# A two-layer transformer kernel: first-stage row stores on GpSimd's queue with three expert buffers, and one 33-row bias product per block

## The reference

```
x = x + L0_attn(layernorm(x), ...)      # 16 heads, bias min(rel * slope, 8), softmax
x = x + L0_xattn(layernorm(x), ctx, mask, ...)
x = x + L0_ffn(layernorm(x), ...)       # top 2 of 8 experts, per sequence
x = x + L1_attn(layernorm(x), ...)      # attends over the 4 sequences at one position
x = x + L1_xattn(layernorm(x), ctx, ...)
x = x + L1_ffn(layernorm(x), ...)       # top 2 of 8 experts, per row
```

## Time and profile before

| | us |
|---|---|
| median of three runs | 3141.96 (3135.05 to 3144.26) |
| the profiled execution | 3139.22 |
| its span in the profile | 3137.4 |
| first stage (`constants`) | 0 to 101.9 |
| first mixture (`mixture0`) | 1293.8 to 1340.7 |
| second self-attention (`attention1`) | 1357.2 to 1460.3 |

### The profile page before, as it was taken

How to read it: one execution, slowest core, us unless ns; L and a number is a source line. 1 busy time by engine, 2 the same in 40 slices (tenths; PEclk the granted TensorE clock), 3 DMA queues, 4 the chain that set the end, 5 groups by cost and what they waited for, 6 DMA issues and landing times. The chain is left out here.

```text
span 3137.4 us, 38375 instructions
## 1 busy us (share of the span) xinstructions
PE 2805.0 (89%) x12634; PEld 1764.7 (56%) x12634; DVE 1855.2 (59%) x3754; ACT 1302.2 (42%) x2326; POOL 1662.9 (53%) x1406
## 2 busy tenths in 40 slices
PE   5688886999999999587999999999999999999979
PEld 5344445555565665454656556665656556556557
DVE  2466766665767665446555556556556555556456
ACT  1155564444455455122444444444444444444410
POOL 2144403665666667502466666666666666666710
PEclk8789998999999999797999999999999999999979
DMA  8655613232332321002223232224222233222110
GB/s 278 132 152 163 157 33 109 64 102 51 103 75 54 97 63 32 34 0 73 60 69 74 53 99 68 52 68 106 53 67 68 54 97 75 57 63 63 32 54 27
DMA packets 114229, 245.51 MB, mean 78 GB/s; under 512 B 16239, under 2 KB 62576, under 8 KB 112881
## 3 DMA queue, kind: packets, MB, share of 16 engines
q1 hardware_dynamic: 107824, 219.52, 27.4%
q0 software_dynamic: 5696, 23.42, 2.7%
q10 hardware_dynamic: 512, 0.13, 0.0%
HBM read 106.98 MB, written 31.80 MB: 44 GB/s over the span
## 5 line engine op out<-in xcount | busy, mean ns | idle before, releaser
L1049 POOL TENSOR_TENSOR ACC<-ACC,PR 128x512 f32<-128x512 f32 (+1 forms) x1056 | 1331.0, 1282 | 456.2 <-ACT PR L1274 448.2
L1274 ACT ACTIVATE PR<-banks 128x512 f32<-128x512 f32 (+1 forms) x832 | 468.8, 597 | 669.2 <-PE banks L1163 668.2
L1335 DVE TENSOR_REDUCE mx<-banks 128x2 f32<-128x800 f32 (+1 forms) x512 | 504.1, 986 | 393.6 <-PE banks L1115 392.0
L1179 PE MATMUL banks<-PR,V 128*64 128x512 f32 (+1 forms) x2496 | 599.1, 604 | 0.0
L1162 PE MATMUL banks<-QA,KA 128*128 128x512 f32 (+1 forms) x1248 | 535.5, 429 | 12.3 <-DMA QB<-ROW 11.5
L1115 PE MATMUL banks<-KH,QZ 128*128 128x400 f32 (+1 forms) x1536 | 480.7, 372 | 41.2 <-DVE mx L1335 20.8
L1163 PE MATMUL banks<-QB,KB 65*128 65x512 f32 (+1 forms) x1248 | 495.2, 397 | 0.0
L1115 PEld LDWEIGHTS banks<-KH,QZ 128*128 128x128 f32 x1536 | 267.9, 189 | 225.6 <-issue 89.7
L1274 ACT ACTIVATE PR<-banks,small 128x512 f32<-128x512 f32 (+1 forms) x416 | 269.4, 687 | 300.3 <-PE banks L1163 290.1
L1332 DVE CUSTOM_DVE_ANT_0 banks<-banks,maskadd 128x400 f32<-128x400 f32 (+1 forms) x512 | 289.2, 588 | 143.6 <-PE banks L1115 136.8
L1303 DVE TENSOR_TENSOR KB<-banks,KH 64x400 fp32r<-64x400 f32 (+1 forms) x384 | 219.4, 571 | 260.0 <-ACT KH L1207 254.5
(11 more groups left out here) (243 smaller groups left out, 2977.4 us busy)
## 6 DMA issues: line engine op xcount, KB each, us to landing
KA<-KH SPq DMA_DIRECT2D x192, 400.5 KB
CX<-ctx_split SPq DMA_DIRECT2D x8, 2403.0 KB, 10.4
WK<-wk_split SPq DMA_DIRECT2D x48, 256.0 KB, 5.7
WV<-wv_split SPq DMA_DIRECT2D x24, 512.0 KB, 3.9
QA<-QZ SPq DMA_DIRECT2D x96, 128.0 KB
QB<-QZ SPq DMA_DIRECT2D x96, 128.0 KB
first<-in_w_in SPq DMA_DIRECT2D x8, 1024.0 KB, 6.2
second<-in_w_out1T SPq DMA_DIRECT2D x8, 1024.0 KB, 8.8
```

The source lines that it names most:

```text
L1049: pool.tensor_tensor(acc, other, PR[0:r, n % RING, :], ALU.add).then_inc(summed, 1)
L1179: last = pe.matmul(OB[h * DH:(h + 1) * DH, :], V[0:r, g % 4, s, h * DH:(h + 1) * DH], PR[0:r, (n + h) % RING, :], start=(s == 0), stop=(s ...
L1274: act.activation(PR[0:r, n % RING, :], SB[n % 3][0:r, :], ACT.Exp, bias=keybias[0:r, g // pairs, t:t + 1] if masked else 0.0).then_inc(pro ...
L1335: dve.tensor_reduce(mx[:, :, t, c], couples[i % 2 if g == 0 else 0][:, :, 0:w], AX.X, ALU.max).then_inc(mx_done, 1)
```

## The change

In the first stage the `tab` load and the ten row stores are issued by GpSimd instead of SyncE; `tab` ahead of the `relb` iotas, the stores behind the selects. The two zeroings go behind the stores, and the row of zeros is then stored from the zeroed `QS`, so `nil` goes. The expert buffers become three pairs: load e waits for expert e - 3, and store e - 3 follows load e in SyncE's order. In the second self-attention the two one-row products per block become one over 33 rows: row 0 of `row_hl` holds the high half, row 32 the low half, the rows between are zeros, and `one_hi` has 33 rows of ones. For that the bias vectors are loaded twice, into partitions 0 and 32, and GpSimd has more to do in the first mixture.

```diff
-                         (self.row1[:, 0:3 * C], row("b1_in")), (self.row1[:, 3 * C:4 * C], row("b1_out"))):
+                         (self.row1[0:1, 0:3 * C], row("b1_in")), (self.row1[0:1, 3 * C:4 * C], row("b1_out")),
+                         (self.row1[32:33, 0:3 * C], row("b1_in")), (self.row1[32:33, 3 * C:4 * C], row("b1_out"))):
...
                 def load_expert(e):
-                    if e >= 2:
-                        sp.wait_ge(ready, e - 1)
+                    if e >= 3:
+                        sp.wait_ge(ready, e - 2)
...
                 load_expert(0)
                 load_expert(1)
+                load_expert(2)
                 sp.dma_start(self.X[:, :, :], a["x"].rearrange("b (t p) c -> p (b t) c", p=P)).then_inc(x_in, 16)
...
-                sp.wait_ge(tabled, 2 * H + NT + 1)
-                sp.dma_start(tab[:, :], table[:, :, :]).then_inc(tab_in, 16)
-                sp.wait_ge(cleared, 4)
-                sp.wait_ge(dstep, 7)
...
-                for e in range(2, E1):
+                for e in range(3, E1):
                     load_expert(e)
-                    store_expert(e - 2)
+                    store_expert(e - 3)
+                store_expert(E1 - 3)
                 store_expert(E1 - 2)
                 store_expert(E1 - 1)
...
+                pool.wait_ge(tabled, 2 * H + NT + 1)
+                pool.dma_start(tab[:, :], table[:, :, :]).then_inc(tab_in, 16)
                 for h in range(BANDS):
                     pool.iota(relb[:, h, :], [[1, P]], base=int(CLAMP[h]), channel_multiplier=-1,
                               allow_small_or_imprecise_dtypes=True).then_inc(related, 1)
...
-                pool.memset(raw(self.QS[:, :, :]), 0.0).then_inc(zeroed, 1)
-                pool.memset(raw(self.KS[:, :, :, :]), 0.0).then_inc(zeroed, 1)
...
+                pool.wait_ge(cleared, 3)
+                pool.dma_start(k_rows[14], one[:, :]).then_inc(z_out, 16)
+                pool.wait_ge(dstep, 7)
+                for i in range(2):
+                    pool.dma_start(k_rows[NT * i:NT * (i + 1)].rearrange("t h n -> (t h) n"), raw(ZK[:, i, :])).then_inc(z_out, 16)
+                    pool.dma_start(k_rows[8 + 3 * i:11 + 3 * i].rearrange("t h n -> (t h) n"), raw(ZK[0:3 * H, 2, :])).then_inc(z_out, 16)
+                pool.wait_ge(dstep, 13)
...
+                pool.memset(raw(self.QS[:, :, :]), 0.0).then_inc(zeroed, 1)
+                pool.memset(raw(self.KS[:, :, :, :]), 0.0).then_inc(zeroed, 1)
+                pool.wait_ge(zeroed, 4)
+                pool.dma_start(q_rows[14], raw(self.QS[0:H, 0, :])).then_inc(z_out, 16)
+                pool.wait_ge(z_out, 16 * 10)
...
-                dve.memset(nil[:, :], 0.0).then_inc(cleared, 1)
...
-                link(pool.tensor_tensor(row[:, 0:3 * C], row[:, 0:3 * C], self.gam1[0:1, :], ALU.mult))
-                link(pool.tensor_tensor(row[:, 3 * C:4 * C], row[:, 3 * C:4 * C], self.gam2[0:1, :], ALU.mult))
-                link(pool.tensor_copy(self.row_hi[:, :], row[:, :]))
-                link(pool.tensor_tensor(self.row_lo[:, :], row[:, :], raw(self.row_hi[:, :]), ALU.subtract))
-                link(pool.tensor_copy(self.one_hi[:, :], self.ones[0:1, :]))
+                hl, hi = self.row_hl, self.row_x
+                link(pool.memset(raw(hl[:, :]), 0.0))
+                for r in (0, 32):
+                    link(pool.tensor_tensor(row[r:r + 1, 0:3 * C], row[r:r + 1, 0:3 * C], self.gam1[r:r + 1, :], ALU.mult))
+                    link(pool.tensor_tensor(row[r:r + 1, 3 * C:4 * C], row[r:r + 1, 3 * C:4 * C], self.gam2[r:r + 1, :], ALU.mult))
+                link(pool.tensor_copy(hl[0:1, :], row[0:1, :]))
+                link(pool.tensor_copy(hi[32:33, :], row[32:33, :]))
+                link(pool.tensor_tensor(hl[32:33, :], row[32:33, :], raw(hi[32:33, :]), ALU.subtract))
+                link(pool.tensor_copy(self.one_hi[:, :], self.ones[0:33, :]))
...
-                    pe.matmul(J, self.one_hi[:, :], self.row_hi[:, o:o + n], start=False, stop=False)
-                    return pe.matmul(J, self.one_hi[:, :], self.row_lo[:, o:o + n], start=False, stop=True)
+                    return pe.matmul(J, self.one_hi[:, :], self.row_hl[:, o:o + n], start=False, stop=True)
...
-                            pe.matmul(J, self.one_hi[:, :], self.row_hi[:, 3 * C:4 * C], start=False, stop=False)
-                            last = pe.matmul(J, self.one_hi[:, :], self.row_lo[:, 3 * C:4 * C], start=False, stop=True)
+                            last = pe.matmul(J, self.one_hi[:, :], self.row_hl[:, 3 * C:4 * C], start=False, stop=True)
```

More of the change, by code:

```diff
@@ L146, in middle_room @@
         self.alpha = sb("alpha", [P, CK])
-        self.row1 = sb("row1", [1, 4 * C])
-        self.row_hi = sb("row_hi", [1, 4 * C], F32R)
-        self.row_lo = sb("row_lo", [1, 4 * C], F32R)
-        self.one_hi = sb("one_hi", [1, P], F32R)
+        self.row1 = sb("row1", [33, 4 * C])
+        self.row_hl = sb("row_hl", [33, 4 * C], F32R)
+        self.row_x = sb("row_x", [33, 4 * C], F32R)
+        self.one_hi = sb("one_hi", [33, P], F32R)
     def norm_all(self, HTA, Hn, ahead=None, low=None):
@@ L238, in constants @@
             one = tmp("one", [H, S])
-            nil = tmp("nil", [H, S])
             work = tmp("work", [TH, 3, S])
@@ L243, in constants @@
             KF = F1 // P
-            first = [tmp(f"first{i}", [P, KF, C]) for i in range(2)]
-            second = [tmp(f"second{i}", [P, KF, C]) for i in range(2)]
+            first = [tmp(f"first{i}", [P, KF, C]) for i in range(3)]
+            second = [tmp(f"second{i}", [P, KF, C]) for i in range(3)]
             parts = tmp("parts", [P, 2, 2, CK * C], F32R)
-            we_in = [sem("w_in0"), sem("w_in1")]
+            we_in = [sem("w_in0"), sem("w_in1"), sem("w_in2")]
             we_out = [sem("w_out0"), sem("w_out1")]
@@ L258, in load_expert @@
                 def load_expert(e):
-                    if e >= 2:
-                        sp.wait_ge(ready, e - 1)
-                    sp.dma_start(first[e % 2][:, :, :], a["w_in1"][e].rearrange("(k p) n -> p k n", p=P)).then_inc(we_in[e % 2], 16)
-                    sp.dma_start(second[e % 2][:, :, :], a["w_out1T"][e].rearrange("(k p) n -> p k n", p=P)).then_inc(we_in[e % 2], 16)
+                    if e >= 3:
+                        sp.wait_ge(ready, e - 2)
+                    sp.dma_start(first[e % 3][:, :, :], a["w_in1"][e].rearrange("(k p) n -> p k n", p=P)).then_inc(we_in[e % 3], 16)
+                    sp.dma_start(second[e % 3][:, :, :], a["w_out1T"][e].rearrange("(k p) n -> p k n", p=P)).then_inc(we_in[e % 3], 16)
                 def store_expert(e):
@@ L297, in _ @@
                     sp.wait_ge(we_out[i], 16 * E1 // 2)
-                sp.wait_ge(z_out, 16 * 10)
                 sp.wait_ge(x_in, 16 * 6)
@@ L327, in _ @@
                                            base=lim, pattern=[[0, P]], channel_multiplier=-1).then_inc(made, 1)
+                k_rows, q_rows = self.k_rows, self.q_rows
+                pool.wait_ge(cleared, 3)
[5 more added lines that the diff above has]
+                pool.wait_ge(dstep, 13)
+                for i in range(2):
+                    pool.dma_start(q_rows[NT * i:NT * (i + 1)].rearrange("t h n -> (t h) n"), raw(ZQ[:, 0, :])).then_inc(z_out, 16)
+                    pool.dma_start(q_rows[8 + 3 * i:11 + 3 * i].rearrange("t h n -> (t h) n"), raw(ZQ[0:3 * H, 1 + i, :])).then_inc(z_out, 16)
+                pool.memset(raw(self.QS[:, :, :]), 0.0).then_inc(zeroed, 1)
[3 more added lines that the diff above has]
+                pool.wait_ge(z_out, 16 * 10)
             @block.scalar
@@ L347, in _ @@
                 for e in range(E1):
-                    pe.wait_ge(we_in[e % 2], 32 * (e // 2 + 1))
+                    pe.wait_ge(we_in[e % 3], 32 * (e // 3 + 1))
                     if e >= 4:
@@ L352, in _ @@
                         for k in range(KF):
-                            last = pe.matmul(bank[e % 4][:, m * C:(m + 1) * C], first[e % 2][:, k, m * P:(m + 1) * P],
-                                             second[e % 2][:, k, :], start=(k == 0), stop=(k == KF - 1))
+                            last = pe.matmul(bank[e % 4][:, m * C:(m + 1) * C], first[e % 3][:, k, m * P:(m + 1) * P],
+                                             second[e % 3][:, k, :], start=(k == 0), stop=(k == KF - 1))
                     last.then_inc(ready, 1)
@@ L1489, in _ @@
                     pool.tensor_tensor(X[:, t, :], X[:, t, :], Hn[:, t, :], ALU.add).then_inc(based, 1)
-                pool.wait_ge(self.att1_in, 16 * 7)
+                pool.wait_ge(self.att1_in, 16 * 9)
                 for k in range(CK):
```

10 lines of the change are left out of this document (removed).

## The result

The changed kernel takes **3113.1 us** (median of 4 runs, 3107.8 to 3116.1) where the kernel before takes 3142.0 us in the same comparison: **ratio 0.991, 95% interval 0.9896 to 0.9924**. A second comparison on another occasion gave 3113.1 us (6 runs) and 0.9911 [0.9895, 0.9927]. The profiled execution took 3112.4 us (span 3110.6). So the forecast of 3115 us held, and 3113 lies inside the range; but none of its three terms came out right for quite the reasons given, and their errors partly cancelled, as the stages show.

The account below looks back on a forecast made before the run. Bounds: late expert loads in the first stage, PE and VectorE in the mixture, TensorE up to a ScalarE copy in the second self-attention. Gains 16.9 + 9.1 - 0.7 = 25.3 us from 3139.2 and 3142.0 gave 3115 us, range 3105 to 3127.

Parts of the forecast that it names:

- 16.9 us forecast: First stage: it would end at 85.0 us instead of 101.9, a gain of 16.9 us, bounds 12.0 to 19.0.
- the stream brings one with its store each 7.9 us, so PE is not the bound: First stage: transfers need 7.9 us per expert with its store, TensorE 7.17 us, so transfers set the pace.
- my 72.3: First stage: the last expert's load would land at 72.3 us (70.2 to 75.5), the mixed transfers taken at 330 GB/s.
- 0.7 us lost forecast: Mixture stage: added GpSimd work would slow a VectorE product on the path by 0.7 us, bounds nothing to 2.34.
- What I called the third: Mixture stage: the VectorE `wbg` product starting at 1325.67 us, claimed to run beside GpSimd after the change.
- 9.1 us forecast: Second self-attention: one bias product per block instead of two gains 7.7 us up to a ScalarE copy plus 1.4 us.
- The bound that I had worked out from the columns alone: Second self-attention: lower bound if only the columns' time is saved, 20 x 0.11 + 10 x 0.22, plus 4 x 0.2: 5.2 us.
- the second step: Second self-attention: TensorE's last four output blocks, at the low clock, each save 0.36 us, 1.4 us together.
- One (holes in the stream): First stage: SyncE's waits come late for each expert, leaving queue holes; only 10 us won there, 3121 us; chance 0.12.
- two (nothing from the product): Second self-attention: the new bias product saves nothing, as weight loads or VectorE's sums set the pace; 3123 us; chance 0.06.
- four (`tab` behind the backlog): First stage: `tab` on GpSimd's queue waits behind SyncE's backlog; stage gains 11 us, 3120 us; chance 0.04.
- Three (the low clock all through the stage): First stage: TensorE stays at the low clock, 14.3 us an expert, stage 27.6 us later, 3158 us; chance 0.03.

Follow-up runs that it names:

- after_again: The changed kernel itself, nothing altered, run and traced once more: 3113.1 us, ratio 0.9911 against the kernel before.
- first_only: The changed kernel with the two one-row bias products brought back, so only the first stage is new: 3120.9 us, ratio 0.9933 against before.
- one_row: The changed kernel with a one-row bias product, the high half alone, the low half left out: 3108.4 us, one run.
- x_late_again: Second run of the changed kernel with six other loads (X, w, wout, biases) moved behind the experts' loads: 3104.0 us, ratio 0.9885 against before.
- bias_only: The changed kernel with the old first stage brought back, so only the bias product is new: 3133.4 us, ratio 0.9971 against before.
- x_late_q: The changed kernel with six other loads behind the experts' loads and the second self-attention's projection bias for the query half alone: 3105.2 us, ratio 0.9889 against before.

## Why the prediction was right, point by point

**First stage: 16.9 us forecast, 18.8 measured; the steps around it right, the bound wrong.** As said: the gap before the third expert gone, a gap of 7.1 (forecast 8.5) before the fourth, table steps from 8.3 us, nine of the ten row stores issued by 18.4, zeroings done by 32.2 (forecast 37), no wait at the rows, queue never empty before 70 us, and a tail of 83.1 - 70.6 = 12.5 us behind the last expert's first product (77.51 - 6.9 = 70.6), forecast 12.7. The failed step is "the stream brings one with its store each 7.9 us, so PE is not the bound". I took 330 GB/s for the mixed part; it ran at 359 to 377 GB/s from 30 to 65 us, where the experts' loads alone had 348, so 2.62 MB took some 7.2 us. The trace of before had shown it, in windows that I left out for one in which the transfers were not always busy (70 to 75 us): here loads beside a store,

```profile
45.00:50.00 5.00, 5.00 (x20) 4.19 (x19) 0.00 (x0) 0.00 (x0) 0.00 (x0) 0.77 1.10 357
```

and 361 GB/s from 40 to 45 us. TensorE needs 6.9 us for an expert inside a run; the 7.17 us that I used is one expert by itself. With rates so near each other the one that starts late decides, and that was TensorE: it had nothing to do from 33.02 to 40.15 us, the granted clock was 0.51 and 0.50 (the low level, 1.2 GHz) from 35 to 45 us, and expert 3 took 9.8 us, as the split behind it shows (ScalarE at 49.92 us). The last expert's second load, issued at 57.23 us and 11.3 us under way, was there at 68.5 us, 3.8 us before my 72.3; TensorE came to it at 70.6. So my stream was too slow by 3.8 us, and 2.1 us of that were lost again because TensorE came late. Expert 3's 2.9 us over the 6.9 cover that: it is the clock, which I had left out. (The gain itself is uncertain by the 1.5 us between the two traces of the old stage.)

**Mixture: 0.7 us lost forecast; about 0.95 lost, on another product, and hidden in the trace by the clock.** The stage has four `wbg` products. What I called the third, at 1325.67 us, is the fourth; the true third was hit:

```profile
1296.91 1.79 POOL L1501 TENSOR_TENSOR row<-row,gam 1x768 f32<-1x768 f32 x1
...
1297.62 2.16 DVE L1571 TENSOR_TENSOR wbg<-wb,small 128x1024 f32<-128x1024 f32 x1
1298.78 1.59 POOL L1502 TENSOR_TENSOR row<-row,gam 1x256 f32<-1x256 f32 x1
1299.84 3.32 PEld L1517 LDWEIGHTS banks<-wbg,wa 128*128 128x128 f32 x16 [3.26 <-DVE wbg L1571]
```

It starts inside GpSimd's 1.79 us and takes 2.16 us instead of 1.21; GpSimd's next, started inside it, takes 1.59 us instead of the 0.72 of the same line four microseconds later. The same pair in the trace of before, where the product began as the multiply ended:

```profile
1314.80 1.79 POOL L1496 TENSOR_TENSOR row<-row,gam 1x768 f32<-1x768 f32 x1
...
1316.58 1.21 DVE L1565 TENSOR_TENSOR wbg<-wb,small 128x1024 f32<-128x1024 f32 x1
1316.67 1.70 POOL L1497 TENSOR_TENSOR row<-row,gam 1x256 f32<-1x256 f32 x1
```

So there the two already met, and only GpSimd paid (1.70 us). The 33-row memset moved the multiply later against VectorE's product. The one that I had named began at 1307.66 us, as the subtract had ended at 1307.65, and took 1.22. My mistake was to skip this product and to lay the new work behind the old in time without sliding the old multiplies themselves. That whichever of the two starts first holds the pair of ports and the other waits is what "SBUF — State Buffer" of the Trainium skill (SBUF: two separate sides) says, and this trace agrees: 0.95 us more, where 1.08 us of the multiply were left. The stage's length, with its norm, fell all the same, from 62.69 to 62.05 us, because TensorE's last L1517 block (L1511 before) ran at the full clock (3.72 us, before 5.41). I don't count that as the change's doing: in after_again, the same kernel, the stage takes 66.20 us. Nor is the 0.95 us a fixed price. In the twelve traces with the longer GpSimd list this product takes from 1.22 to 2.16 us, in after_again 1.30: there TensorE's blocks ahead of it, and with them the product, came later against GpSimd's list, and a later GpSimd multiply paid (2.67 us instead of 1.80).

**Second self-attention: 9.1 us forecast, 7.9 measured; the mechanism right, the size taken at the wrong end.** Up to the resume I had 7.7 us, from the distance between the two products' starts, 0.22 and 0.33 us. What a product gives back when it is taken away is 0.11 and 0.22: the 0.40 us in front of it stays with the one that is left. The bound that I had worked out from the columns alone, 20 x 0.11 + 10 x 0.22 = 4.4 us, was the value: 4.6 measured. Behind the resume the second step failed: 1.4 us was forecast, for four products at the low clock, and the stretch became 3.6 us shorter (44.86 to 41.24). All of it lies in the last four output blocks. From the resume to the first of them it is 32.38 us in both traces, and from its start to the end of the last one 10.98 us before and 7.36 after:

```profile
1447.83 2.07 PE L1657 MATMUL banks<-wo,AT 128*128 128x256 f32 x4 [0.69 <-ACT AT L1693]
```
```profile
1423.88 2.07 PE L1662 MATMUL banks<-wo,AT 128*128 128x256 f32 x4 [0.69 <-ACT AT L1697]
```

The bias products of these four blocks in the changed kernel; one of them shows the longer product of the low clock:

```profile
1425.89 0.58 PE L1663 MATMUL banks<-row_hl,one_hi 33*128 33x256 f32 x1
1428.12 0.38 PE L1663 MATMUL banks<-row_hl,one_hi 33*128 33x256 f32 x1
1429.49 0.38 PE L1663 MATMUL banks<-row_hl,one_hi 33*128 33x256 f32 x1
1430.86 0.38 PE L1663 MATMUL banks<-row_hl,one_hi 33*128 33x256 f32 x1
```

where before all four do (0.58 each; one in the earlier trace rows). Against first_only, with the old products and the new first stage, the gain of the stage is 8.2 us. The earlier rise of the clock goes with the new product: the stretch takes 44.9 and 45.2 us in the two traces with the old pair (before, first_only), 41.2 to 41.5 us in seven with the new product or with `one_row`'s, and 42.6 in two more (after_again, x_late_again). `bias_only` is among the seven, with 41.3; its expectation had asked whether this part of the gain was chance. Why the clock rises there isn't shown, and it isn't a matter of shorter blocks alone: `x_late_q`, with the shortest, takes 44.0.

**The sum.** 18.8 + 7.9 - 0.95 = 25.8 us against 25.3 forecast and 28.3 (24 to 33 by the interval) measured. The errors of the terms, +1.9, -1.2 and -0.25 us, nearly cancelled, and within the 7.9 so did -3.1 up to the resume and +2.2 behind it (the other -0.3 is in the norm, which was that much longer). That the total came within 2 us of the forecast is thus partly luck; the remaining 2.5 us lie inside the interval, and no run gives them a cause.

**The rivals.** One (holes in the stream) fell with the windows above; two (nothing from the product) with 4.6 us at the resume and bias_only's 9.1; four (`tab` behind the backlog) with 8.32 us, though the landing did take 5.7 us for 0.8 KB, all but 0.43 us of it hidden by the strip's clearing. Three (the low clock all through the stage) fell, but its mechanism was there, for the expert behind the pause. I had excluded it by the run after 18.46 us of idle, two experts in 15.79 us. Now that an expert inside a run is known to take 6.9 us, that row reads 8.9 + 6.9: the cost stood in it.

## What to carry to other kernels

Work out the bound of a stage from both sides: where transfers and TensorE need nearly the same time for a unit, a rate that is a few per cent off names the wrong bound, and what delays the start of the later one (here loads that nobody needed yet) is worth more than either rate. A small product that is removed gave back its columns here, not its duration nor the distance to its neighbour's start; ask whether the fixed part (0.40 us here) goes too, which here was so only when the last such product of the block went. And when work is added ahead of other work on GpSimd, slide the whole list and look for each VectorE operation on the path that now falls inside a GpSimd one.

## What the runs showed of the hardware that was not expected

- The changed kernel's transfers moved 359 to 388 GB/s in each window from 15 to 65 us, where the loads of experts and `X` alone had 348. Stores are not the only reason: in before 384 GB/s were moved from 20 to 22 us, when `X` ended and `w` came and no store had been issued.
- A 0.8 KB load on GpSimd's queue, issued while large loads filled the transfer engines, took 5.7 us to land, and the row stores of 32 to 128 KB took 5.1 to 5.9 us in the median of each kind: hardly a matter of size.
- A bias product costs 0.40 us for a block and 0.11 us for each 256 columns, whatever its rows (1 or 33) and in either kind of product; plain fp32 pays the columns four times.
- The first expert after idle time of 6.6 us or more took 8.7 to 10.1 us where one inside a run takes 6.9; in the changed kernel, behind 7.14 us of idle, the granted clock was at 0.51 and 0.50 from 35 to 45 us. For the very first expert the clock column doesn't show it: it has 1.00 from 10 to 15 us, yet 14 products stand in that window of the changed kernel and 25 in one inside a run.
- The mixture stage with its norm took 62.05 us in one trace of the changed kernel and 66.20 us in the other. A stage of 60 us can't be compared between two traces to better than some 4 us without looking at its clock, block by block.
